# Turning a sequence's queries and keys on VectorE in four blocks, with a shorter low-rank split and moved weights

## The reference

```python
x = x + ffn0(cond0(x))                 # a 32x32 mix per sequence, then a 4-bit quantised 512x512 product
# layer 1: attention, 32 query heads, 8 key heads, 128 wide, over a cache of 16 pages of 32 keys plus 32 new keys
q, k, v = x @ Wq.T, x @ Wk.T, x @ Wv.T
q, k = rope(rmsnorm(q, qw), pos), rope(rmsnorm(k, kw), pos)
p = softmax(where(valid, q @ [k_cache, k].T * scale, -1e30))
a = (p @ [v_cache, v]) @ Wo.T
x = x + base(a) + delta(a)             # 512x512 product and a routed low-rank term, top 1 of 4
x = x + ffn2(cond2(x))                 # per-sequence low-rank adapter, then a gated product with rank-2 terms
x = x + ffn3(cond3(x))                 # top-2 routed low rank, then an int8 quantised product
```

## Time and profile before

| | us |
|---|---|
| median of 3 runs | 3076.71 |
| lowest, highest | 3074.37, 3078.14 |
| the profiled execution's own time | 3076.38 |
| its span, first to last instruction | 3074.7 |
| granted TensorE clock, mean | 0.987 of full |

### The profile page before, as it was taken

The page is one execution under the profiler, slowest core; times in us unless marked ns, Lnnn a source line. Parts: engine busy times, 40 slices in busy tenths (PEclk is TensorE's granted clock), DMA queues, the critical chain, the costliest instruction groups (busy, mean ns, idle before and its releaser), DMA issues. The chain is left out here.

```text
span 3074.7 us, 54713 instructions
## 1 busy us (share of the span) xinstructions
PE 2931.6 (95%) x14616; PEld 1941.9 (63%) x14624; DVE 1527.6 (50%) x4189; ACT 1241.4 (40%) x2633; POOL 1459.5 (47%) x1262
## 2 busy tenths in 40 slices
PE   5889999999999999999999999999999998799997
PEld 3566666666666666666666666666666665455554
DVE  4544444444444444444444444444444444577675
ACT  2444444444444444444444444444444442122222
POOL 4555555555555555555555555555555551000000
PEclk9999999999999999999999999999999999899998
DMA  8544444444444444645444444444444444321110
GB/s 304 182 118 122 121 122 121 122 121 121 121 121 121 121 121 121 203 121 166 131 121 121 121 121 121 119 121 119 121 119 120 121 119 149 98 46 53 41 43 14
DMA packets 433387, 369.66 MB, mean 120 GB/s; under 512 B 90598, under 2 KB 371178, under 8 KB 432186
## 3 DMA queue, kind: packets, MB, share of 16 engines
q1 hardware_dynamic: 377834, 187.06, 21.5%
q0 software_dynamic: 48320, 165.48, 16.9%
q10 hardware_dynamic: 7056, 14.53, 1.3%
HBM read 335.66 MB, written 22.81 MB: 117 GB/s over the span
## 5 line engine op out<-in xcount | busy, mean ns | idle before, releaser
L558 DVE CUSTOM_DVE_ANT_0 ps_s<-ps_s,mask 128x544 f32<-128x544 f32 x512 | 374.9, 732 | 931.6 <-PE ps_s L388 919.3
L463 ACT ACTIVATE ps_s<-ps_s,nmax 128x544 f32<-128x544 f32 x512 | 352.3, 688 | 870.6 <-DVE nmax L558 868.4
L288 POOL DMA_INDIRECT v_sb<-in_v_rows_w,v_row x504 | 488.3, 969 | 449.6 <-PE ps_oT L416 240.5
L347 PE MATMUL ps_t<-wqkv,xT 128*128 128x512 f32 x1488 | 700.5, 593 | 0.0
L411 PEld LDWEIGHTS ps_oT<-pT,v_sb 128*128 128x128 f32 x4096 | 528.7, 192 | 192.6 <-issue 174.9
L411 PE MATMUL ps_oT<-pT,v_sb 128*128 128x128 f32 x4096 | 544.7, 276 | 12.9 <-DMA v_sb<-in_v_rows_w,v_row 12.8
L371 PE MATMUL ps_t<-wo,oT 128*128 128x512 f32 x1024 | 521.9, 594 | 1.5 <-ACT oT L477 1.2
L387 PE MATMUL ps_s<-k_sb,qT 128*128 128x416 f32 x1024 | 447.3, 519 | 19.1 <-issue 12.4
L569 DVE TENSOR_SCALAR p_sb<-ps_s,rinv 128x512 f32<-128x512 f32 x512 | 384.5, 751 | 26.9 <-DVE rinv L566 0.3
L396 PEld LDWEIGHTS ps_pT<-ident_sb,p_sb 128*128 128x128 f32 x2048 | 251.8, 141 | 187.5 <-issue 184.1
L347 PEld LDWEIGHTS ps_t<-wqkv,xT 128*128 128x128 f32 x1488 | 254.4, 191 | 178.0 <-issue 178.0
(11 more groups left out here) (224 smaller groups left out, 3305.5 us busy)
## 6 DMA issues: line engine op xcount, KB each, us to landing
k_sb<-in_kT SPq DMA_DIRECT2D x2048, 64.0 KB
v_sb<-in_v_rows_w,v_row POOLq DMA_INDIRECT x512
wo<-in_wo_w POOLq DMA_DIRECT2D x2, 4096.0 KB, 14.5
v_new<-v_raw SPq DMA_DIRECT2D x512, 16.0 KB, 1.8
y_scratch<-y_sb SPq DMA_DIRECT2D x32, 256.0 KB, 2.3
xT<-x1T_scratch POOLq DMA_DIRECT2D x31, 256.0 KB, 4.9
wqkv<-in_wqkv_w ACTq DMA_DIRECT2D x6, 1024.0 KB, 12.2
wqkv<-in_wqkv_w POOLq DMA_DIRECT2D x6, 1024.0 KB, 12.8
```

The costliest lines, as they stand in the source:

```text
L288: e.indirect_dma_start(out=v_sb[:, b % 2, c, :], out_offset=None, in_=A["v_rows_w"], in_offset=bass.IndirectOffsetOnAxis(ap=v_row[:, b, c: ...
L347: m = e.matmul(ps_t[bank_of(t)][:, :], xT[:, k, :], wqkv[:, k, 512 * t:512 * t + 512], start=k == 0, stop=k == KC - 1)
L463: e.activation(scores(u), scores(u), ACT.Exp, bias=nmax[:, u % 2:u % 2 + 1], scale=-1.0, accum_out=rsum[:, u % 2:u % 2 + 1]).then_inc(expe ...
L558: e.tensor_tensor_reduce(out=scores(u), in0=scores(u), in1=mask[:, b % 2, :], scale=-SCALE, scalar=3e38, op0=ALU.add, op1=ALU.min, accum_o ...
```

## The change

- `turn_q` and `copy_q` go from the rounds. VectorE turns the next round's `rot` itself, in blocks of 32 by 32 elements: instruction `turn` takes the 32 rows of one sequence b and 32 columns of each of the 20 heads, and writes them as 32 rows of the new buffer `qkT`. Four instructions make one sequence, 16 a round. `TURN_AT` says how many come in each unit before and after `norm`: eight in units 11 to 15 of the round before, eight in units 0 to 2 of the round itself. Waits on `q_turned` count these. Round 0 is still turned by TensorE in `embed`.
- `rotate` part 0 works tile by tile (4 heads at a time) up to the multiplication by the norm; its later steps are as before.
- In the last round the output product of round 30 goes two heads a unit in units 2 to 9; that of the last round moves into `tail` (11 heads, the transposes of a, 5 heads), its result stored from there. Its transposed input lies in `o_last`, in the room of `wqkv`.
- The six loads of the first half's `wqkv` move from ScalarE's queue to SyncE's, one in each of groups 0 to 5. The constants' block goes; its loads are issued behind those of x. In `embed` VectorE unpacks the 4-bit weights ahead of the first `spread`.
- Round 16's projection waits once for all six weight tiles of the second half.
- In `tail` GpSimd issues the weight loads, some at once, those into the room of `wo` after the output product. VectorE waits for the former before `route`, for the latter before the first step. `split` of both matrices and the two waits change places.
- `split_low_rank` loses two of seven steps: the mask and the matrix of the product ahead of it now carry the other half, so that the sum arrives in PSUM. Two small copies prepare that matrix once.

```diff
-STEPS, STEPS1 = 15, 6
+STEPS, STEPS1, RSTEPS = 17, 8, 8
+TURNS = D // S
+
+
+def blocks_turned(r, b):
+
+
+    return NQT + TURNS * GB * (r - 1) + TURNS * (b + 1)
...
+        self.qkT = sb("qkT", [P, GB, HT, S], F32)
...
+    for t0, t1 in ((0, 1), (1, 2), (2, 3)) if i == 0 else ((3, NQT),):
+        a, b = 4 * t0, 4 * t1
+        e.wait_ge(W.summed, NQT * r + t1)
+        e.sem_inc(W.passed, 1)
+        e.tensor_scalar(ss[:, a:b], ss[:, a:b], 1.0 / D, EPS, ALU.mult, ALU.add).then_inc(rstd_step, 1)
+        e.wait_ge(rstd_step, powers + 1)
+        e.tensor_tensor(rstd[:, a:b], ss[:, a:b], mhalf[:, a:b], ALU.pow).then_inc(rstd_step, 1)
+        powers = powers + 2
+        e.wait_ge(rstd_step, powers)
+        e.wait_ge(W.raw_copied, NT * r + t1)
+        e.tensor_tensor(raw[:, a:b, :], raw[:, a:b, :], rstd[:, a:b].unsqueeze(2).broadcast_to([P, b - a, D]), ALU.mult).then_inc(rope_step, 1)
+        done = done + 1
...
-            e.wait_ge(W.q_turned, NQT * r)
+            e.wait_ge(W.q_turned, blocks_turned(r - 1, GB - 1) if not (isinstance(r, int) and r == 1) else NQT)
...
-    TURN_AT = {8: 0, 9: 1, 10: 2, 11: 3, 12: 4}
+
+
+    TURN_AT = {11: (1, 1), 12: (1, 1), 13: (1, 0), 14: (1, 1), 15: (1, 0), 0: (1, 2), 1: (1, 2), 2: (1, 1)}
+    TURN_NEXT = sum(sum(TURN_AT[u]) for u in range(11, 16))
     OUT_AT = {6: (0, 2), 7: (2, 4), 8: (4, 5), 9: (5, 7), 10: (7, 8), 11: (8, 10), 12: (10, 11), 13: (11, 13), 14: (13, 14), 15: (14, 16)}
+    LAST_OUT_AT = {u: (2 * u - 4, 2 * u - 2) for u in range(2, 2 + HQH // 2)}
...
-                    if is_(r, GROUPS):
-                        e.wait_ge(dma_wqkv[1][t], 16)
+                    if is_(r, GROUPS) and t == 0:
+                        e.wait_ge(dma_wqkv, 16 * NT)
...
-            def turn_q(r, t):
-
-                e.wait_ge(rope_step, STEPS * r + STEPS1 if t < 3 else STEPS * (r + 1))
-                if t == 0:
-                    e.wait_ge(summed, NQT * (r + 1))
-                else:
-                    e.wait_ge(q_copied, NQT * r + t)
-                for h in range(4):
-                    m = e.transpose(ps_t[1][:, h * P:(h + 1) * P], rot[:, 4 * t + h, :], ident[:, :])
-                m.then_inc(q_turned, 1)
...
+                    if first(r):
+                        e.wait_ge(q_copied, NQT)
+                    else:
+                        e.wait_ge(q_turned, blocks_turned(r, b))
...
-                to = oT[:, i, :, :]
+                to = o_last if last(r) else oT[:, i, :, :]
...
+            def turn(r, m):
+
+                b, j = divmod(m, TURNS)
+                rows, at = slice(S * b, S * b + S), slice(S * j, S * j + S)
+                if m == 0:
+                    e.wait_ge(rope_step, STEPS * (r + 1))
+                if j == 0:
+                    e.wait_ge(scored, UNITS * (r - 1) + HKH * (b + 1))
+                    e.wait_ge(placed, GB * (r - 1) + b + 1)
+                e.transpose(qkT[at, b, :, :], rot[rows, :, at]).then_inc(q_turned, 1)
+
+            def turns(r, u, part):
+                if u not in TURN_AT or first(r) and u < 11 or last(r) and u >= 11:
+                    return
+                units = range(11, u) if u >= 11 else range(u)
+                m = (0 if u >= 11 else TURN_NEXT) + sum(sum(TURN_AT[v]) for v in units) + part * TURN_AT[u][0]
+                for n in range(m, m + TURN_AT[u][part]):
+                    turn(r + 1 if u >= 11 else r, n)
...
+                    turns(r, u, 0)
                     if ahead(r, u, 2) is not None:
                         norm(*ahead(r, u, 2))
+                    turns(r, u, 1)
...
+                if g in WEIGHTS_AT:
+
+                    for t in WEIGHTS_AT[g]:
+                        at = slice(512 * t, 512 * t + 512)
+                        e.dma_start(wqkv[:, :, at], A["wqkv_w"][0][:, :, at]).then_inc(dma_wqkv[t], 16)
...
-            e.wait_ge(bd_zero, 1)
-            spread(0)
             e.wait_ge(dma_q, 16 * 5)
             step(e.tensor_scalar(qw, qw, sh[:, 0:1], 15, ALU.logical_shift_right, ALU.bitwise_and))
             zv = zz.rearrange("p g (c j) -> p g c j", j=NIB)
             for j in range(NIB):
                 m = e.tensor_scalar(zv[:, :, :, j], qz, 4 * j, 15, ALU.logical_shift_right, ALU.bitwise_and)
             step(m)
+            e.wait_ge(bd_zero, 1)
+            spread(0)
...
+            e.wait_ge(o_copied, 1)
+            e.dma_start(y_d[ROUNDS - 1, :, :], outb[1][:, :]).then_inc(stored[1], 16)
...
+        @block.gpsimd
+        def _(e):
+            for p in both:
+                e.dma_start(A2g[p][:, :, TR0:P], A["c_w2f"][:, :, P + TR0:FOLDED]).then_inc(dma_low, 16)
+            for n in AT_ONCE:
+                e.dma_start(w[n][:], A["c_" + n]).then_inc(dma_w, 16)
+            e.wait_ge(o_done, 1)
+            for n in AFTER_OUT:
+                e.dma_start(w[n], A["c_" + n]).then_inc(dma_after, 16)
...
-                if first(k):
-                    e.wait_ge(dma_w, REST)
-                    e.wait_ge(setup, 4)
...
+                    e.wait_ge(dma_w, 16 * len(AT_ONCE))
+                    e.wait_ge(dma_after, 16 * len(AFTER_OUT))
...
+            out_product(0, 11)
             e.wait_ge(dma_beside, 16 * len(BESIDE))
-            e.wait_ge(padded, 1)
+            e.wait_ge(padded, 3)
             for p in both:
                 turn_a(0, p)
+            out_product(11, HQH)
             for p in both:
...
-                step(e.tensor_copy(td[p][own, :], bank[p][2][own, 0:P]))
-                step(e.tensor_tensor(td[p][own, :], td[p][own, :], bank[p][2][own, P:2 * P], ALU.add))
-                step(e.tensor_copy(ts[p][own, :], td[p][own, :]))
-                step(e.scalar_tensor_tensor(td[p][own, :], ts[p][own, :], part(0), td[p][own, :], ALU.mult, ALU.add))
+                t = bank[p][2][own, P:2 * P]
+                step(e.tensor_copy(ts[p][own, :], t))
+                step(e.scalar_tensor_tensor(td[p][own, :], ts[p][own, :], part(0), t, ALU.mult, ALU.add))
...
+            split(b1x, b1s)
             sum_halves(0)
-            split(b1x, b1s)
+            split(b3x, b3s)
+            e.wait_ge(dma_w, 16 * len(AT_ONCE))
+            e.tensor_copy(langf[:, :], langi[:, :]).then_inc(setup, 1)
+            e.tensor_copy(qwb[:], q8[:].rearrange("p k n -> p (k n)").bitcast(I8).rearrange("p (k n) -> p k n", k=KC)).then_inc(setup, 1)
             route(0)
-            split(b3x, b3s)
             for p in both:
                 second(0, p)
-            e.wait_ge(dma_w, REST)
-            e.tensor_copy(langf[:, :], langi[:, :]).then_inc(setup, 1)
-            e.tensor_copy(qwb[:], q8[:].rearrange("p k n -> p (k n)").bitcast(I8).rearrange("p (k n) -> p k n", k=KC)).then_inc(setup, 1)
             e.wait_ge(setup, 4)
             sum_halves(1)
...
-        with nc.Block() as block:
-            @block.sync
-            def _(e):
-                e.dma_start(ident[:, :], A["ident"]).then_inc(dma_const, 16)
-                e.dma_start(iota[:, :], A["iota"]).then_inc(dma_const, 16)
-                e.wait_ge(dma_const, 32)
```

132 lines of the change are left out of this document (58 added, 74 removed).

## The result

The changed kernel takes 2962.7 us (median of 4 runs, 2959.6 to 2964.9), the kernel before 3075.5 (median of 4, 3072.8 to 3078.1). The ratio is 0.9632 with the interval 0.9616 to 0.9649: 113 us, or 3.7%, faster. The prediction said 2967 us, with a range from 2945 to 3008. The profiled execution of after has a span of 2960.7 us. One execution of e2 ran at a granted clock of 0.84 and took 3366 us, and its profile is of that one; all ratios are of the others.

A forecast was written before the change was run, and what follows sets the result against it. The prediction took TensorE's instruction stream to bound the rounds, with long idle gaps at both ends. Its terms, -66 + 2 - 2 + 1 + 4.5 - 27 - 9.5 - 12 = -109, took 3076.4 to 2967 us, range 2945 to 3008.

The forecast's parts named there:

- Point 1: Rounds: removing TensorE's five transpose groups saves 2.2 us a round over 30 rounds, -66 us.
- Point 2: Rounds: VectorE's turns take 0.86 us, room 1.17; GpSimd's rotation comes 2.9 us sooner; +2 us (0 to 12).
- Point 3: Round 0: the gather that TensorE awaits comes 2.9 us earlier, and turns fill short units; -2 us (-5 to +2).
- Point 4: Round 16's projection: one wait for all six weight tiles may partly show; +1 us (0 to 5).
- Point 5: Last round: units without an output-product head become longer on VectorE; +4.5 us (+2 to +8).
- Point 6: From attention to the tail's first gates: output product covers loads and a split; -27 us (-15 to -31).
- Point 7: Tail's steps: two split steps fewer remove TensorE's waits for the split; -9.5 us (-7 to -10).
- Point 8: First stage: earlier first load, unpacking first and spread weight loads; -12 us (-5 to -14).
- Ends give half: First stage and attention-to-tail passage: other loads come late, so gains are 20 us rather than 39; 2987 us, chance 15%.
- The gather takes the place: Rounds: without a shorter GpSimd part 0, TensorE waits up to 2.2 us each for block 3; 3033 us, chance 7%.
- Middling turns: Rounds: VectorE's turns cost 1.17 to 1.4 us, each 0.1 beyond 1.17 adding 50 us; 3022 at 1.28, chance 7%.
- slower: Units 11 to 2: VectorE becomes the bound from 1.39 us a turn; 3240 us at 1.72, chance 5%.

The follow-up runs named there:

- e2: Changed kernel with three unused semaphore increments per unit of TensorE's loops (1784 instructions instead of 1688), on the first chip; 2967.6 us, ratio 0.9641.
- e3: Changed kernel with one turn moved from unit 11 to the end of unit 10, on the first chip; 2949.5 us, ratio 0.9582.
- e10: Changed kernel with the six first weight loads issued at once from ScalarE, not spread over the first stage, on the first chip; 2957.6 us, ratio 0.9612.
- e12: Changed kernel with the six first weight loads still spread over groups 0 to 5 but issued by ScalarE, on the first chip; 2947.0 us, ratio 0.9577.
- e6: Same edit as e2 to the changed kernel, repeated on the second chip; 2980.0 us, ratio 0.9676.
- e4: Changed kernel with GpSimd normalising and rotating part 0 in one piece, as before the change, on the first chip; 3031.8 us, ratio 0.9862.
- e11: e3 with the output product spread over units 0 to 10 of the last round and the weights' wait in two groups of three tiles; 2947.9 us, ratio 0.9583.
- e8: Changed kernel with the old low-rank split of seven steps and the old mask, on the second chip; 2977.8 us, ratio 0.9672.
- e7: Changed kernel with each VectorE turn done twice, first into a buffer nobody reads, on the second chip; 3121.2 us, ratio 1.0132.
- e1: Changed kernel with the rounds' transposes given back to TensorE and their copies to ScalarE, on the first chip; 3014.8 us, ratio 0.9801.
- e5: Changed kernel unaltered, run again on the second chip; 2964.4 us, ratio 0.9633.
- e9: Changed kernel with a small unread power on GpSimd ahead of block 3's gather in each round, on the first chip; 2955.5 us, ratio 0.9606.

## Why the prediction was right, point by point

**What bounds the kernel.** Right. In the clean rounds of e3, e10 and e12 TensorE still waits for nothing, with the turns on VectorE.

**Point 1, the transposes, -66.** Right in size and way: 2.18 us a round by the clean rounds, 65.4 in 30. What the point left out is the loop around them. The 86 instructions a pass by which before's loop of TensorE is longer decide whether it is fetched anew; the same step, by 96 increments, is worth 15 us in e6. The rows were there to be seen: ten waits at the start of the rounds with no releaser, in the waits of before, 145 to 2577 us:

```profile
PE ps_s L387 <- issue: 12.4, 10, 1.5
```

**Point 2, the turns, +2.** The turn takes 0.836 us where 0.86 was taken from the one-element rate of the earlier trace rows; the bounds 0.43 and 1.72 both fell. The figures of the Trainium skill gave an estimate of 0.84 (VectorE: DVE Perf Modes, "The three transpose paths", with Vector Engine (DVE) Microarchitecture Reference, section 3.8): the trace agrees. The working of unit 14 that left a slack of 0.16 us holds where the signal is on time: 5.9 us of waits for `p_sb` in e3, 6.4 in e12, for all rounds together. In after the late signal starts VectorE's run 2.6 us late in 26 rounds, and 30 rounds are 13.2 us longer than e12's (2259.3 against 2246.1). So the term of +2 was 6 at most in e3 and e12, and 15 to 20 where after was measured (26 rounds at 0.75 are 19.5). This is the step that failed: it counted VectorE's idle time as free anywhere in units 11 to 2, and took for granted that a signal comes at once.

The misses in the rounds are thus -15 for the fetching and +13 for the signal, and they cancel: -65.4 - 14.9 + 13.2 is -67.1, and -67.4 was measured. The sum of the rounds was right, then, partly by luck.

**GpSimd's part in point 2** (2.9 us sooner against 2.2 us wanted sooner) was right, and e4 shows what hung on it.

**Point 3, round 0, -2.** -4.8, inside its bounds. The wait for the gather is there yet, 3.98 instead of 5.22 us:

```profile
172.93 2.08 PE L416 MATMUL ps_oT<-pT,v_sb 128*128 128x128 f32 x8 [3.98 <-DMA v_sb<-in_v_rows_w,v_row]
```

**Point 4, one wait for six tiles, +1.** Rounds 14 and 15 take 154.0 us in after, 5.2 over two clean ones; in before they took 159.2, 6.0 over. So it cost nothing. In before TensorE waited 3.24 us for the gather there, as the prediction's "spares one for the gather" has it; in e3 it is 4.2 us for the weights instead, in after 2.82 us without a releaser. Two groups (e11) gave 2.0 beside e3.

**Point 5, last round, +4.5.** +5.5, for the reason given: units without output product are VectorE's. e11 brought 3.3 of it back by giving nearly every unit a head.

**Point 6, -27.** -25.9. TensorE's timeline of after, from the last weighing to the gates, answers to the earlier trace rows:

```profile
2501.17 1.06 PE L421 MATMUL ps_oT<-pT_new,v_new 128*128 128x128 f32 x8
...
2506.06 11.38 PE L1245 MATMUL c_ps<-wo,wqkv 128*128 128x512 f32 x22 [3.84 <-PEq L226]
2517.28 1.04 PE L1252 MATMUL c_ps<-ident_sb,c_a 128*128 128x128 f32 x8
2518.15 4.46 PE L1245 MATMUL c_ps<-wo,wqkv 128*128 128x512 f32 x10
...
2533.63 0.66 PE L1252 MATMUL c_ps<-ident_sb,c_x 128*128 128x128 f32 x4
...
2541.17 1.42 PE L1323 MATMUL c_ps<-wqkv,c_sT 128*128 128x344 f32 x4
```

The idle 8.56 and 16.53 us are gone: the last product now covers the loads of a, and both splits lie beside other work. 38.9 us against 39.3 worked out, but with other parts. The block change is 3.8 instead of 2, as at the start of the kernel. The work from the product's end to the gates is 18.6 instead of some 22. It no longer stands behind gaps: the granted clock is 0.96 from 2502 to 2541 us, where in before it was 0.76 between 2577 and 2642, a mean of time at TensorE's two levels, 1.2 and 2.4 GHz, in a stretch with two long pauses.

**Point 7, the tail, -9.5.** -13.4; e8 alone gives 12.5 to 13.3. Waits that the profile lists were all counted; 0.3 us a step before the first split of a pair was below what it lists.

**Point 8, first stage, -12.** -7.9 in after, -9.4 by the mean of the nine runs named under e10, in which the first score comes at 104.2 to 106.9 us (after is 1.5 above that mean). The spreading brought its 6 (e10). The constants and the order brought 3.4 of 6. At TensorE's first mix, which waits for `spread`, only 2.4 us of those 6 are there, first before, then after:

```profile
18.98 2.07 PE L786 MATMUL ps_y<-bd,xa 128*128 128x128 f32 x8 [18.98 <-DVE bd L951]
```

```profile
16.54 2.08 PE L806 MATMUL ps_y<-bd,xa 128*128 128x128 f32 x8 [16.54 <-DVE bd L967]
...
49.77 2.08 PE L806 MATMUL ps_y<-bd,xa 128*128 128x128 f32 x8 [4.05 <-DMA xa<-in_x_w]
```

The two gains were added, but `spread` now stands on VectorE behind the unpacking, so both can't be won for it. Yet that doesn't settle the stage either: the second mix is 7.0 us earlier than in before and the fifth 15.0, then TensorE waits for x, as in the last line, and from the eighth mix on it is some 8 us ahead. So the loads of x in the middle of the stage decide what remains, as the rival of the ends had it; which of the gains they swallow wasn't tried.

**The rivals.** *Ends give half*: not so; 25.9 + 7.9 = 33.8 of the 39 us came, where the rival had 20, though its reason shows in the first stage. *The gather takes the place*: it does as soon as GpSimd's part 0 is whole (e4), to within 2 us of its price. *Middling turns* and *slower*: not at 0.836 us. With 1.67 us a turn e7 became slower than before, as the point of 1.39 said it would, though at 6.0 us a round over a clean one of 74.41 instead of the (1.67 - 1.17) x 16 = 8.0 of that working; VectorE's idle time beyond the half that was reckoned as within reach must have taken the rest, which is argued from the sum alone. The rule that a 128x128 turn belongs on TensorE (the Trainium skill, VectorE: DVE Perf Modes, "Rules for kernel authors") would have cost here: e1 follows it and takes 52 us more than after, and 65 more than e3 on its own chip.

**What stays open** is the cause of the late signal, and with it how much the change is worth on a given chip. Known is that it comes in 23 to 27 rounds of after, e5, e6 and e8, always at unit 13 while SyncE issues keys and GpSimd gathers, and in no run of the first chip, whatever the edit. SyncE's slower issuing is there in e7 too, where VectorE has one such wait, of 1.2 us, so it can come without the late signal. Whether the chip decides, and whether a moved turn or gather would remove the signal where it occurs, no run tells: the changed kernel on the first chip, or e3, e9 and e12 on the second, would have.

## What to carry to other kernels

When one engine is without waits, work moved from it to an engine that idles is won in full, but only with its neighbours: ask for each chain behind the moved work (here rotation and gather) by how much sooner it is wanted, and shorten it in the same change. Look at the instruction queue's packets and at gaps with no releaser at the start of a loop; a long unrolled body may be just over what stays fetched. Run the unaltered kernel in every group of experiments, on its chip: without it e3, e9, e10 and e12 each seemed to have found a cure. Check a sum by its parts against undisturbed rounds, since a total can be right with two errors in it.

## What the runs showed of the hardware

- TensorE's loop of 1774 or 1784 instructions (two rounds) is fetched again when it starts over: 136 to 138 packets on the instruction queue, 0.9 to 1.8 us idle at ten places in before, e1 and e6, about 1.5 us net for each in e6. One of 1688 is not (46 packets, no such gap). Where between them the bound lies, and how far the other engines' loops count, wasn't tried.
- VectorE's turn of 32x32 blocks in 4-byte floats, 32 partitions by 640 elements, takes 836 ns: per element the rate of the sum over 512 in the earlier trace rows, 687 ns.
- A semaphore's count from TensorE reached VectorE 2.6 us late, in 26 rounds of 31, in a stretch in which SyncE took about 10 us instead of 8.3 for sixteen loads. It was seen in after and on the second chip, and never on the first, there not even with the same instructions (e2 against e6).
